# Moving GpSimd's small steps and VectorE's block maxima inside one pass of a fused attention and FP4 kernel

## The reference, cut to what matters

```python
def fp4_quant_dequant(x):          # blocks of 16 along the last dim
    scale = max(|block|) / 6       # at least 1e-12
    q = nearest of {0, .5, 1, 1.5, 2, 3, 4, 6} to |block / scale|
    return q * sign * scale

xn = layernorm(x)
s  = attention(xn)                 # Gram matrix of a batch, 256 x 256, with q/k norms
h  = silu(fp4(xn) @ fp4(w_gate).T) * (fp4(xn) @ fp4(w_up).T)      # 704 columns
g  = silu(fp4(h) @ fp4(w_down).T)
out = x + s * g
```

## Time and profile before

| what | value |
|---|---|
| three runs | 672.07, 673.58, 677.53 us (median 673.58) |
| profiled execution, its own time | 670.61 us |
| its span on the core | 668.8 us |
| mean granted TensorE clock | 0.971 of full speed |
| busy: PE, DVE, ACT, POOL | 578.5, 592.5, 420.7, 292.5 us |

### The profile page before, as it was taken

One profiled execution on the slowest core, in us unless ns is written; L12 is line 12 of the kernel. 1 busy time (PEld: TensorE's weight loads), 2 busy tenths in 40 slices (PEclk: granted clock), 3 DMA queues, 4 the chain that ended last, 5 costly groups with the idle time before them and its releaser, 6 DMA issues.

```text
span 668.8 us, 15805 instructions
## 1 busy us (share of the span) xinstructions
PE 578.5 (87%) x5139; PEld 444.0 (66%) x5139; DVE 592.5 (89%) x1263; ACT 420.7 (63%) x1046; POOL 292.5 (44%) x224
## 2 busy tenths in 40 slices
PE   0147789999999889999998889999998999998857
PEld 0134567676767667778877667778776777776646
DVE  7987999988999999989999989999999998878544
ACT  3157888866768777666866567666866686534220
POOL 5423345432563445534744444534753453215226
PEclk9966999998999999999999989999998999999799
DMA  7001010000000101111110111111110101040023
GB/s 239 0 16 33 18 33 17 17 19 16 18 17 33 33 1 49 49 48 50 48 49 1 63 38 49 49 48 50 48 50 18 63 21 32 16 141 32 32 79 127
DMA packets 17762, 29.43 MB, mean 44 GB/s; under 512 B 2704, under 2 KB 5136, under 8 KB 17680
## 3 DMA queue, kind: packets, MB, share of 16 engines
q1 hardware_dynamic: 17680, 28.39, 12.4%
HBM read 19.99 MB, written 8.39 MB: 42 GB/s over the span
## 4 chain that ended last, share of the span: by engine, by line
PE 38%; DVE 35%; issue 15%; ACT 5%; POOL 4%; DMA 1%; DVEq 1%; POOLq 0%; SPq 0%; ACTq 0%
PE GU L1342 16%; DVE hg L882 5%; PE DS L1352 4%; DVE hq L890 4%; PE G L1406 4%; DVE ham L849 3%; DVE xq L831 3%; DVE h L842 3%; PE DS L1354 2%; PE TR L1295 2%; POOL ht L530 2%; DVE st L796 2%; PE GU L1362 2%; ACT sil L597 1%; PE G L1425 1%
## 5 line engine op out<-in xcount | busy, mean ns | idle before, releaser
L1342 PE MATMUL GU<-wgu,xqT 128*128 128x352 f16 x1536 | 255.1, 317 | 7.7 <-ACT xnT L613 4.4
L1342 PEld LDWEIGHTS GU<-wgu,xqT 128*128 128x128 f16 x1536 | 148.3, 99 | 83.0 <-ACT xnT L613 4.6
L597 ACT ACTIVATE sil<-GU,wkap 128x352 f32<-128x352 f32 x128 | 70.9, 554 | 82.7 <-PE GU L1342 79.6
L530 POOL TENSOR_TENSOR ht<-h,hrr 128x1408 f32<-128x1408 f32 x32 | 82.8, 2588 | 65.8 <-DVE hrr L856 65.8
L842 DVE SCALAR_TENSOR_TENSOR h<-GU,wkap,sil 128x352 f32<-128x352 f32 x128 | 70.7, 553 | 32.5 <-ACT sil L597 28.8
L490 POOL TENSOR_TENSOR xnat<-xs,xnat 128x512 f16<-128x512 f32 (+1 forms) x32 | 37.4, 1168 | 120.4 <-DVE ht L879 104.5
L1352 PE MATMUL DS<-wdT,hqT 128*128 128x256 f16 x704 | 88.1, 274 | 1.3 <-ACT hqT L604 1.3
L1352 PEld LDWEIGHTS DS<-wdT,hqT 128*128 128x128 f16 x704 | 67.3, 99 | 10.6 <-ACT hqT L604 1.5
L497 POOL TENSOR_TENSOR xt<-xs,xrr 128x512 f32<-128x512 f32 x32 | 34.0, 1062 | 89.8 <-DVE hq L890 87.1
L890 DVE TENSOR_TENSOR hq<-hg,hs 128x704 f16<-128x704 f16 x128 | 64.5, 545 | 0.8
L543 POOL TENSOR_TENSOR o<-y,xe 128x512 f32<-128x512 f32 x25 | 35.9, 1437 | 60.4 <-DVE y L901 33.6
(11 more groups left out here) (177 smaller groups left out, 1101.8 us busy)
## 6 DMA issues: line engine op xcount, KB each, us to landing
xin<-in_L_attn_x SPq DMA_DIRECT2D x34, 256.0 KB, 2.7
xe<-in_L_attn_x SPq DMA_DIRECT2D x25, 256.0 KB, 2.8
out<-o SPq DMA_DIRECT2D x25, 256.0 KB, 2.1
h<-in_L_ffn_w_down SPq DMA_DIRECT2D x1, 704.0 KB, 6.9
gring<-in_L_ffn_w_gate SPq DMA_DIRECT2D x1, 640.0 KB, 4.4
gring<-in_L_ffn_w_up SPq DMA_DIRECT2D x1, 640.0 KB, 5.5
xs<-in_L_attn_x SPq DMA_DIRECT2D x2, 256.0 KB, 3.8
xt<-in_L_attn_x SPq DMA_DIRECT2D x2, 256.0 KB, 4.3
```

The lines of the kernel that those rows point to most:

```text
L530: g.tensor_tensor(paired(ht[:, 0:2 * I]), paired(h[:, q]), spread(hrr[:, q], 4 * CB), ALU.mult).then_inc(S["ht_d"], 1)
L597: a.activation(sil[:, c], GU[:, c, 0, 0:CH], ACT.Silu, scale=wkap[:, 0:1]).then_inc(S["sil_d"], 1)
L1342: last = t.matmul(GU[:, c, m, 0:CH], xqT[:, k, j, 2 * a_ + kc], wgu[:, b_, kc, 2 * m + c], start=(z == 0 and kc == 0), stop=(z == 2 and kc ...
```

## The change

GpSimd's order in an iteration becomes: `ht`, wait for `hw_d`, `x_rstd`, `o`, wait for the first `hloq` of the pair, `x_low`, wait for the second `hloq`, `x_divide`, `norm_products` if due. VectorE takes the maxima of x (part 0) behind the third h pass instead of in the first half of the iteration, part 1 behind `h_round` part 1 instead of ahead of part 0, and the reciprocal (part 2) behind the fourth h pass instead of ahead of the third. ScalarE takes `x_high` behind its fourth silu instead of ahead of it. No instruction is added or removed.

```diff
 (GpSimd, iteration)
                 last_batch = isinstance(b, int) and b == BATCHES - 1
+                if on["xa"] and on["mb"]:
+                    wait(pool, "hw_d", p)
+                if on["xf"]:
+                    x_rstd(p + 1)
                 if on["o"]:
                     e, ko = p - LAGE - 1, (k + LAGE + 1) % 2
...
                 if on["xa"]:
                     if on["mb"]:
-                        wait(pool, "hw_d", p)
+                        wait(pool, "hloq", 2 * p - 1)
                     x_low(p, k)
-                if on["xf"]:
-                    x_rstd(p + 1)
+                    if on["mb"]:
+                        wait(pool, "hloq", 2 * p)
+                    x_divide(p, k)
                 if i == 2:
                     norm_products(b)
-                if on["xa"]:
-                    if on["mb"]:
-                        wait(pool, "hloq", 2 * p)
-                    x_divide(p, k)
 (ScalarE, iteration)
+                if on["m"]:
+                    silu(p, 1, 1)
                 if on["xa"]:
                     x_high(p, k)
-                if on["m"]:
-                    silu(p, 1, 1)
 (VectorE, iteration)
                     x_front(p + 1, 1 - k)
-                if on["xa"]:
-                    x_scales(p, k, 0)
...
                     x_round(p, k, 1)
-                if on["xa"]:
-                    x_scales(p, k, 1)
                 if on["xb"]:
                     x_scales(p - 1, 1 - k, 3)
                 if on["mb"]:
                     h_round(p, k, 0)
-                if on["xa"]:
-                    x_scales(p, k, 2)
                 if on["m"]:
                     h_mul(p, k, 1, 0, i)
                 if s_beside(p, 1, tail):
                     e_half(p, k, 1, 0)
+                if on["xa"]:
+                    x_scales(p, k, 0)
                 if on["xb"]:
                     x_round(p, k, 2)
                 if on["mb"]:
                     h_round(p, k, 1)
+                if on["xa"]:
+                    x_scales(p, k, 1)
                 attention(1, 0)
...
                     h_mul(p, k, 1, 1, i)
                 if s_beside(p, 1, tail):
                     e_half(p, k, 1, 1)
+                if on["xa"]:
+                    x_scales(p, k, 2)
                 attention(1, 1)
```

More of the change, by code:

```diff
@@ L545, in iteration @@
                     if on["mb"]:
-                        wait(pool, "hw_d", p)
+                        wait(pool, "hloq", 2 * p - 1)
                     x_low(p, k)
-                if on["xf"]:
-                    x_rstd(p + 1)
-                if i == 2:
-                    norm_products(b)
-                if on["xa"]:
                     if on["mb"]:
@@ L557, in iteration @@
                     x_divide(p, k)
+                if i == 2:
+                    norm_products(b)
                 if i == (2 if last_batch else 3):
```

## The result

The changed kernel takes **691.6 us** (median of four runs, 688.2 to 694.5), the kernel before 672.8 (four runs, 670.5 to 677.5): a ratio of 1.0268, 95% interval 1.0184 to 1.0352. It is slower, as forecast, but by 18 us over the 673.6 from which the forecast counted, where 9 were forecast, and 1.6 us above the top of the range; the four runs are 688.2, 688.8, 694.4 and 694.5, so two of them lie inside it. The profiled execution took 688.2, the shortest of the four, with a span of 686.4 us beside 668.8 before: 17.6 us to explain. Lines of `after` behind the moved GpSimd code are 2 higher than before: L890 is now L892, L831 L833, L872 L874, L806 L808, L809 L811, L1295 L1297.

What follows compares the result with a forecast made beforehand. TensorE and VectorE, both nearly full, each set part of a batch; the chain through VectorE, GpSimd and ScalarE sets the head. Terms 2.2 + 4.0 + 2.8 = 9.0 on 673.6 gave 682.6 us, range 667 to 690.

Steps and rivals of the forecast that it cites:

- The head: Pairs 1 to 5: net +1.0 a pair on the VectorE chain slips TensorE over pairs 2 to 4; +2.2 us.
- The products: Norm products after `x_divide` delay `ht`: TensorE slips 1.6 in pairs 16 and 24, 0.8 in pair 8; +4.0 us.
- Where VectorE sets the pace: Loop pairs 9-12, 17-20, 25-28: old stalls exchanged for holds on L831 or L882 and L890; +0.95 a batch, +2.8 us.
- the first rival: Pairs 17 to 20: VectorE's wait for the third silu covers `o`, saving 10.2 in all; 666 us, chance 0.15.
- Elsewhere in the loop TensorE is the bound and VectorE's later half is hidden in its waits for silus: Loop pairs outside those VectorE paces: the moved work adds no time; no term in the sum.
- The forecast's reading of the earlier trace: In the loop TensorE waits almost only for VectorE's attention-chain answers: 1.8 us for `mtop`, 1.5 us for `Mx`.
- `x_high` at no cost: ScalarE's `x_high` waits for part 1, some 3 us after the fourth silu; ScalarE's idle 5.7 a pair covers it.
- the rival that it reaches TensorE: ScalarE's wait in `x_high` reaches TensorE through `rows_out`, 1 us in nine pairs more; 692 us, chance 0.08.
- The mode table: At L831 and L890: `tensor_tensor` has no two-port mode, so the 1.2 and 0.45 us stalls would be nothing.
- the forecast's second rival: L831 and L890 not held at all: 1.65 in each of nine turns goes, 15 us; 668 us, chance 0.02.

Runs made afterwards that it cites:

- experiment 3: The changed kernel with the norm products put back ahead of `x_divide`; 689.0 us, 1.0244 to the kernel before.
- 1: The kernel before with only the change's VectorE and ScalarE half, GpSimd's order as before; 679.8 us, 1.0086 to the kernel before.
- experiment 5: The changed kernel with ScalarE's `x_high` moved behind the second `g_out`; 690.7 us, 1.0269 to the kernel before.
- experiment 6: The changed kernel with `x_low` alone put back behind the third h pass, ahead of `x_rstd`; 689.6 us, 1.0247 to the kernel before.
- 7: The changed kernel with the output sum `o` alone put back right behind `ht`; 687.3 us, 1.0215 to the kernel before.
- 11: The changed kernel with `x_low` back behind the third h pass and the norm products back ahead of `x_divide`; 686.2 us, 1.0202 to the kernel before.
- 2: The kernel before with only the change's GpSimd half, VectorE and ScalarE in their old orders; 684.5 us, 1.0187 to the kernel before.
- experiment 4: The changed kernel with the maxima of x put back into the first half; 685.7 us, 1.0188 to the kernel before.
- experiment 8: The kernel before with the maxima of x moved behind the first `x_round` where `o` is on; 673.2 us, 0.9996 to the kernel before.

## Why the forecast fell short

The direction came true and so did most single readings. The sum did not: one step put five pairs at nothing, one term was half of what it measured, and a change of the clock was in no term.

- **The head, 2.2 forecast, 2.7 measured.** The mechanism is right: L892 at 1.37, L824 standing beside `ht`, 15.06 us a pair where 15.2 was said. The nearness of the sum is partly luck: pairs 1 to 5 grew 3.29, as pair 1 and pair 5 grew too (0.48 and 0.30), and the lag of -0.59 that pair 0 began with hides it.
- **The products, 4.0 forecast, 4.25 measured.** `ht` came 1.58 later where 1.6 was said, and TensorE waited where it should. The step's other half, that the last L890 gains 1.0 and loses 1.0 to stalls and moved scales, agrees with experiment 3: with the products first again only 0.95, 0.49 and 0.49 us come back, and the rest stays with the other moves. In the first batch it is 1.41 where 0.8 was forecast.
- **Where VectorE sets the pace, 2.8 forecast, 5.3 measured: mis-sized.** The stall moved, as said, but mostly not to L831 or L882: `o` lost its turn to them and held L811, and in two pairs of a batch only (1.09 us in 18 and in 19, the same in 26 and 27); in pair 20 it held the first L833 for 0.6. Pairs 17 and 20 have the silu wait of the first rival (1.25 and 0.48). The largest part that was not foreseen is pair 10, 1.82 us, where a longer wait for `mtop` was followed by the lower clock.
- **"Elsewhere in the loop TensorE is the bound and VectorE's later half is hidden in its waits for silus": this step failed.** It costs 3.3 us in pairs 6, 13, 14, 21 and 22. The later half is hidden as far as the third silu; what lies between that silu and an answer that TensorE waits for is not. The maxima make the three `nrm` waits 2.0 us longer in all, but not all of that reaches the time. In pairs 14 and 22 it does: the lag grows 0.62 to 0.67 each in the runs with the maxima late (the change, 1, 3, 5, 6, 7, 11) and 0.11 to 0.16 in those with them early (2, 4), so about 1.0 us is shown. The other 2.3, in pairs 6, 13 and 21, stay open: they do not go when the maxima go back (experiment 4). The forecast's reading of the earlier trace rows, that TensorE waits almost only for the attention chain, also left out the longest wait of that view, 2.1 us for `y` (L901) at 394.02; the changed kernel has 1.9 at the same place.
- **`x_high` at no cost: right,** against the rival that it reaches TensorE (experiment 5).
- **The mode table.** The table of the Trainium skill, Advanced Engine Details and Errata, section VectorE Performance Modes, gives `tensor_tensor` no two-port mode; read by itself, as the forecast's second rival read it, L831 and L890 would not be held. The rows say otherwise again: L892 1.37 beside `x_low`, 0.89 in experiment 6 where `x_low` lies elsewhere. The Trainium skill, SBUF — State Buffer, section Who interferes with whom, has it as the rows do: `tensor_tensor` with both inputs in SBUF contends with GpSimd's reads, and `tensor_scalar`, which L811 is, can contend under conditions.
- **Pairs 30 and 31, 1.6 us,** are a stretch at 1.2 GHz that no term of the forecast held; of the runs with parts of the change five show it at that place (1, 4, 5, 6, 7) and three do not (2, 3, 11). What decides it is open.

## What to carry to other kernels

An instruction that is moved from in front of a wait to behind it is new work on the chain behind that wait, even if the engine's total stays the same: 0.67 us of maxima made each `nrm` wait 0.68 us longer, and about 0.5 of it reached the time in pairs 14 and 22. Moving the GpSimd instruction mostly moved the stall between it and VectorE (experiments 6 and 7); putting an instruction beside it that is not held made the stall smaller (experiment 8: the reduction of 0.67 us beside `o`, L872 0.85 instead of 1.45), but that instruction must not be the filler of another wait. The longest wait on a list (48 us of `x_high`) can cost nothing; take it away before you blame it.

## What the runs showed of the hardware that was not expected

- A held GpSimd instruction does not always get in between two of VectorE's: in the earlier trace rows a product starts between the two of L890, but in pair 18 above `o`, listed at 380.07, waits through two of L833 and one of L884. Its listed 3.43 us are then mostly waiting; in pairs without a hold it is listed with 1.27.
- VectorE's `tensor_scalar` on 32 numbers a partition (L811) is held like the operations with two inputs, 1.26 instead of 0.17.
- TensorE's granted clock fell to 0.50 behind a 2.93 us wait in pair 10 and stayed at 1.00 behind 2.32 us (194.71) of the same run; but experiments 6 and 7 have 0.50 behind the same wait of pair 8 (2.31 and 2.32), and the kernel before has 0.50 behind 1.77 us and 1.00 behind 1.78. In pairs 6 and 30 of the changed kernel it fell with TensorE busy, behind the small matmuls of L1436 and idle times there of 0.69 and 0.45 us. Experiment 5, whose times are those of the changed kernel, had the same stretches, in pairs 6, 10 and 30.
